# Feed-forward attention: the weighted values between the first two score tiles, the whole output product behind the fourth row's turns, the fourth score tile last

## What is computed

```
q = (h @ wq + bq).reshape(S, N_HEADS, HEAD_DIM)        # and kk, v; then the rotation
att = jnp.einsum('shd,thd->hst', q, kk) / np.sqrt(HEAD_DIM)
att = jnp.where(causal[None], att, jnp.finfo(att.dtype).min)
att = jax.nn.softmax(att, axis=-1)
attn_out = jnp.einsum('hst,thd->shd', att, v).reshape(S, N_HEADS * HEAD_DIM) @ wo
x1 = x + attn_out
h2 = _rms_norm(x1, ln2_w)
mlp = jax.nn.silu(h2 @ w_gate) * (h2 @ w_up) @ w_down
```

## Time and profile before

| | |
|---|---|
| median of 3 runs | 1528.08 us (1525.26 to 1529.14) |
| the profiled execution's own time | 1524.64 us |
| its span in the profile | 1522.9 us |
| TensorE busy | 1497.2 us, 98% |
| VectorE busy | 1182.6 us, 78% |
| ScalarE busy | 715.8 us, 47% |
| GpSimd busy | 688.5 us, 45% |
| attention of the second layer | scores from 1249 us on, the last output product until 1393 us |

### The profile page before, as it was taken

One profiled execution on the slowest core, in us unless ns is written; L12 is line 12 of the kernel. 1 busy time (PEld: TensorE's weight loads), 2 busy tenths in 40 slices (PEclk: granted clock), 3 DMA queues, 4 the chain that ended last, 5 costly groups with the idle time before them and its releaser, 6 DMA issues.

```text
span 1522.9 us, 41381 instructions
## 1 busy us (share of the span) xinstructions
PE 1497.2 (98%) x16220; PEld 1186.7 (78%) x16220; DVE 1182.6 (78%) x1884; ACT 715.8 (47%) x1458; POOL 688.5 (45%) x727
## 2 busy tenths in 40 slices
PE   8999999999999999999999999999999999999997
PEld 6777777777777777777777777777777787778997
DVE  6765788888888888888888888888887686554986
ACT  5874444444444444444444444444445124655431
POOL 3543344454444454444444444544445692114752
PEclk9999999999999999999999999999999999999999
DMA  8961121211111221112221112121125524010000
GB/s 262 346 207 60 39 63 52 77 56 50 56 54 59 67 66 50 56 50 62 62 70 50 56 50 62 58 75 50 56 87 154 196 111 167 28 56 29 1 1 25
DMA packets 70199, 121.04 MB, mean 79 GB/s; under 512 B 21840, under 2 KB 36528, under 8 KB 68608
## 3 DMA queue, kind: packets, MB, share of 16 engines
q1 hardware_dynamic: 69312, 117.54, 23.9%
q0 software_dynamic: 832, 2.75, 0.7%
HBM read 89.93 MB, written 30.34 MB: 79 GB/s over the span
## 4 chain that ended last, share of the span: by engine, by line
PE 89%; DVE 5%; ACT 3%; issue 1%; DMA 1%; POOL 1%; ACTq 0%; DVEq 0%; POOLq 0%
PE ps L1535 21%; PE ps L1536 19%; PE ps L1537 18%; PE ps L1691 10%; PE ps L1654 6%; PE ps L1625 3%; PE ps L1596 3%; PE ps L1660 2%; PE ps L1900 2%; PE ps L1917 2%; PE ps L1909 1%; PE ps L1664 1%; DMA q_dram<-q_turned 1%; DVE rec L1163 1%; PE ps L1636 0%
## 5 line engine op out<-in xcount | busy, mean ns | idle before, releaser
L547 POOL TENSOR_TENSOR ctx_lo<-ctx_raw,ctx_hi 128x472 fp32r<-128x472 f32 (+1 forms) x62 | 112.8, 1819 | 192.8 <-ACT ctx_hi L780 192.8
L1163 DVE RECIPROCAL rec<-ps 128x224 f32<-128x224 f32 x128 | 198.3, 1549 | 1.1 <-PE ps L1691 0.9
L581 POOL TENSOR_TENSOR prob_img<-prob 128x448 f32<-128x448 f32 x93 | 107.9, 1160 | 149.3 <-ACT prob L845 149.3
L1152 DVE TENSOR_REDUCE top<-ps 112x4 f32<-112x1028 f32 x128 | 156.2, 1220 | 0.0
L1151 DVE TENSOR_REDUCE top<-ps 112x4 f32<-112x472 f32 x128 | 83.1, 649 | 72.9 <-PE ps L1625 72.9
L1654 PE MATMUL ps<-q_all,k_all 32*128 32x112 f32 (+1 forms) x3072 | 125.2, 274 | 0.0
L1535 PE MATMUL ps<-w_v_img_hi,ctx_hi 128*128 128x512 f32 x256 | 107.4, 419 | 0.0
L1535 PE MATMUL ps<-w_k_img_hi,ctx_hi 128*128 128x512 f32 x256 | 107.1, 418 | 0.0
L843 ACT ACTIVATE prob<-ps 119x448 f32<-119x448 f32 x96 | 52.4, 546 | 114.8 <-PE ps L1654 114.8
L1654 PEld LDWEIGHTS ps<-q_all,k_all 32*128 32x128 f32 (+1 forms) x3072 | 105.4, 184 | 0.0
L1536 PE MATMUL ps<-w_k_img_lo,ctx_hi 128*128 128x512 f32 x256 | 101.1, 395 | 0.0
(11 more groups left out here) (358 smaller groups left out, 4410.7 us busy)
## 6 DMA issues: line engine op xcount, KB each, us to landing
ctx_raw<-in_ctx_dram SPq DMA_DIRECT2D x32, 748.0 KB, 4.2
xh_dram<-xh SPq DMA_DIRECT2D x32, 448.0 KB
xc<-in_xT_dram SPq DMA_DIRECT2D x28, 256.0 KB, 4.5
q_dram<-q_turned SPq DMA_DIRECT2D x28, 256.0 KB, 4.6
q_all<-q_dram SPq DMA_DIRECT2D x32, 224.0 KB, 3.1
out_dram<-out_sb SPq DMA_DIRECT2D x32, 224.0 KB, 2.3
xh<-in_x_dram SPq DMA_DIRECT2D x31, 224.0 KB, 2.9
proj<-in_x_dram SPq DMA_DIRECT2D x21, 256.0 KB, 5.1
```

The lines of the kernel that those rows point to most:

```text
L547: nc.gpsimd.tensor_tensor(ctx_lo[:, :, cols], ctx_raw[:, :, cols], ctx_hi[:, :, cols].bitcast(F32), ALU.subtract).then_inc(ctx_lo_done, 1)
L581: nc.gpsimd.tensor_tensor(prob_img[:, g % 2], image[:, 0, :], image[:, 1, :], ALU.add).then_inc(img_summed, 1)
L1152: nc.vector.tensor_reduce(rows[:, :, 2 * g + 1], ps[0:L, 2:6, TAIL:CTX], AX.X, ALU.max).then_inc(s_done, 1)
L1163: nc.vector.reciprocal(rec[:], bank[:, 2:4]).then_inc(norm_step, 1)
```

## The change

It writes the same instructions in another order, on three engines; none is added or removed.

TensorE, heads from 2 on: `weigh(h - 2)` goes from before the first score tile to between the first and the second. The turn of the second tile of the head before goes ahead of the first score tile, and the turn of the first tile ahead of the fourth score tile, which comes last. The output product stays one piece behind the turn of the fourth tile.

The diff:

```diff
--- before.py
+++ after.py
@@ -1046,32 +1046,53 @@
                     act.wait_ge(down_step, j - 2)
                 nc.scalar.activation(m_hi[:, j % 3, :], m_prod[:, j % 2, :], ACT.Copy).then_inc(m_hi_done, 1)
 
-            for k in range(FH * NC + LAG + 2):
-                if k % NC == 0 and k >= 2 * NC:
-                    attn_rounded(k // NC - 2)
-                if LAG <= k < FH * NC + LAG:
+            def prob_exp(k):
+                c = k % NC
+                n_keys = (c + 1) * L
+                act.wait_ge(top_ready, k + 1)
+                if k < AMONG:
+                    act.wait_ge(head_ready, NHEAD - 2 * AMONG + k + 1)
+                if k > LAG:
+                    act.wait_ge(pT_full, k - LAG)
+                nc.scalar.activation(prob2[:, k % (LAG + 1), 0:n_keys], ps[0:L, 4 + k % 2, 0:n_keys], ACT.Exp, bias=neg_top[:, c:c + 1],
+                                     accum_out=prob_sum[:, c:c + 1]).then_inc(prob_ready, 1)
+
+            for k in range(2 * NC):
+                if k >= LAG:
                     turn_evac(k - LAG)
-                if k < FH * NC:
-                    c = k % NC
-                    n_keys = (c + 1) * L
-                    act.wait_ge(top_ready, k + 1)
-                    if k < AMONG:
-                        act.wait_ge(head_ready, NHEAD - 2 * AMONG + k + 1)
-                    if k > LAG:
-                        act.wait_ge(pT_full, k - LAG)
-                    nc.scalar.activation(prob2[:, k % (LAG + 1), 0:n_keys], ps[0:L, 4 + k % 2, 0:n_keys], ACT.Exp, bias=neg_top[:, c:c + 1],
-                                         accum_out=prob_sum[:, c:c + 1]).then_inc(prob_ready, 1)
-                if k == 24:
+                prob_exp(k)
+                if k == NC + 2:
+                    wo_rounded(0)
+            attn_rounded(0)
+            prob_exp(2 * NC)
+            turn_evac(2 * NC - 3)
+            for h in range(2, FH):
+                k = NC * h
+                if h >= 3:
+                    turn_evac(k - 3)
+                    prob_exp(k)
+                    attn_rounded(h - 2)
+                if h == 6:
                     act.wait_ge(gate_step, NC)
                     nc.scalar.activation(gate_e[:], sel_score[:], ACT.Exp, scale=-1.0).then_inc(gate_exp, 1)
-                if k % NC == 2 and 1 <= k // NC <= FH:
-                    wo_rounded(k // NC - 1)
-                if k == FH * NC + LAG:
-                    act.wait_ge(att_full, FH * NC)
-                    act.wait_ge(ring_loaded[0], 48)
-                    act.wait_ge(ring_loaded[1], 32)
-                    gate_up_rounded(0)
-                    gate_up_rounded(1)
+                prob_exp(k + 1)
+                turn_evac(k - 2)
+                prob_exp(k + 2)
+                wo_rounded(h - 1)
+                turn_evac(k - 1)
+                turn_evac(k)
+                prob_exp(k + 3)
+            turn_evac(FH * NC - 3)
+            attn_rounded(FH - 2)
+            turn_evac(FH * NC - 2)
+            turn_evac(FH * NC - 1)
+            wo_rounded(FH - 1)
+            act.wait_ge(att_full, FH * NC)
+            act.wait_ge(ring_loaded[0], 48)
+            act.wait_ge(ring_loaded[1], 32)
+            gate_up_rounded(0)
+            gate_up_rounded(1)
+            attn_rounded(FH - 1)
 
             for kc in range(KC):
                 at = FH + FKV + KC + kc
@@ -1437,10 +1458,13 @@
 
             for k in range(FH * NC + LAG + 3):
                 c = k % NC
+                sooner = c in (0, 3) and k >= 2 * NC + 3
+                if sooner and k <= FH * NC:
+                    scale_probs(k - 1)
                 if k < FH * NC:
                     dve.wait_ge(att_full, k + 1)
                     nc.vector.tensor_reduce(neg_top[:, c:c + 1], ps[0:L, 4 + k % 2, 0:(c + 1) * L], AX.X, ALU.max, negate=True).then_inc(top_ready, 1)
-                if 1 <= k <= FH * NC:
+                if 1 <= k <= FH * NC and not sooner:
                     scale_probs(k - 1)
                 if k < 2:
                     rope(NHEAD - AMONG + k)
@@ -1936,23 +1960,33 @@
                     last.then_inc(o_step, 1)
 
             pe.wait_ge(consts2, 2)
-            for k in range(FH * NC):
-                if k % NC == 0 and k >= 2 * NC:
-                    weigh(k // NC - 2)
+            for c in range(AMONG):
+                att(c)
+                project_head(NHEAD - AMONG + c)
+            turn_probs(0)
+            for k in range(NC, 2 * NC):
                 att(k)
-                if k < AMONG:
-                    project_head(NHEAD - AMONG + k)
-                if k >= LAG:
-                    turn_probs(k - LAG)
-                if k % NC == 2 and 2 * NC <= k < FH * NC - NC:
-                    output_T(k // NC - 2)
-                elif k == FH * NC - 2:
-                    output_T(FH - 3, first)
+                turn_probs(k - LAG)
+            weigh(0)
+            att(2 * NC)
+            turn_probs(2 * NC - 3)
+            for h in range(2, FH):
+                k = NC * h
+                if h >= 3:
+                    turn_probs(k - 3)
+                    att(k)
+                    weigh(h - 2)
+                att(k + 1)
+                turn_probs(k - 2)
+                att(k + 2)
+                turn_probs(k - 1)
+                output_T(h - 2, range(KC) if h < FH - 1 else first)
+                turn_probs(k)
+                att(k + 3)
+            turn_probs(FH * NC - 3)
             weigh(FH - 2)
-            turn_probs(FH * NC - 3)
-            output_T(FH - 3, range(2, 3))
             turn_probs(FH * NC - 2)
-            output_T(FH - 3, range(3, KC))
+            output_T(FH - 3, second)
             turn_probs(FH * NC - 1)
             output_T(FH - 2, first)
             weigh(FH - 1)
```

## The result

| | before | changed |
|---|---|---|
| median | 1526.81 us (1525.26 to 1529.14, 4 runs) | 1546.26 us (1544.81 to 1548.0, 4 runs) |
| profiled execution | 1524.64 us | 1544.97 us |
| span | 1522.9 us | 1543.2 us |

What follows compares the result with a forecast made beforehand. TensorE, busy 1497.2 of 1522.9 us, was taken as the bound. Terms 16.1 + 1.0 - 0.4 gave +16.7 us: 1541.3 from the profiled 1524.64, 1544.8 from the median 1528.08; forecast 1544.5 us, range 1538 to 1550.

Steps and rivals of the forecast that it cites:

- The mechanism: In each head, ScalarE's three-block copy waits behind the second tile's exponential; the four-block turn waits 1.66 us instead of 0.15.
- 13 periods: From the first head's output product to the loop's last: 13 heads, each 1.24 us longer, together 16.1 us.
- The first output product: Ahead of the first output product the copy is held once, so it starts later: +1.0 us.
- Behind the loop: After the loop, the weighted values between two turns cover a head's two old waits: -0.4 us, an estimate.
- The clock: TensorE's granted clock in the attention stage was to stay 1.00, 2.4 GHz, adding nothing.
- Rival (c): TensorE's clock falls to 1.2 GHz for a tenth of 14 heads' matmul work: 1555 us, chance 0.05.
- Ahead of the stage: Before the feed-forward attention stage nothing was to move by more than 1 us.
- (a): In each head `attn_hi` starts 0.28 us sooner, wait 1.38: +0.96 a head, +13.1 in all, 1541 us; chance 0.11.
- (b): ScalarE's three-block copy isn't held, four-block wait stays 0.15: 3.9 us gained, 1524 us, or 1522 without that wait; chance 0.06.

Runs made afterwards that it cites:

- the first experiment: Changed kernel with ScalarE's copy of the three-block turn ahead of the second tile's exponential again, also before the loop: 1525.96 us, ratio 0.9993.
- the better order: Changed kernel with each ScalarE copy of a turn ahead of the next exponential and VectorE's order as before: 1522.75 us, ratio 0.9976.
- VectorE's edit undone: Changed kernel with the fourth tile's scaling behind the first tile's maximum again on VectorE: 1541.75 us, ratio 1.0096.
- the rest repaired: Changed kernel with ScalarE's copy ahead of the exponential everywhere except where the first output product waits for it: 1529.92 us, ratio 1.0024.
- ScalarE alone: Kernel before with only ScalarE's loop as changed, TensorE and VectorE as before: 1553.74 us, ratio 1.0196.
- the maximum ahead: Changed kernel with the second tile's maximum taken ahead of `attn_lo` on VectorE, ScalarE's order as changed: 1532.75 us, ratio 1.004.

## Why the prediction was right, and where it was off

*The mechanism held, step by step.* From the fourth tile's mask (1339.08) the prediction had the first tile's exponential at 2.55, `attn_hi` at 2.90, `attn_lo` at 3.48, the maximum at 4.01, the exponential at 4.43, the copy at 4.87, the four-block turn at 5.46. Measured: 2.53, 2.88, 3.44, 3.99, 4.40, 4.84, 5.42. TensorE was ready at 3.80, as worked out. The wait is 1.62 for 1.66, the head 9.14 for 9.17. The experiments show each link: with the copy moved the wait goes (0.18), with `attn_lo` moved it is 0.73, with the scaling moved 1.41.

*The terms of the sum*, for the two profiled executions, which differ by 20.3 us:

- 13 periods: 16.1 predicted, 13 x 1.21 = 15.7 measured.
- The first output product: +1.0 predicted; from the first score tile to its start 22.75 us before and 23.77 after, +1.0.
- Behind the loop: -0.4 predicted, about -0.6 measured (second product to the MLP's first matmul +13.9, less 12 periods, 14.5).
- **The clock: 0 predicted, +1.6 measured.** This is the step that failed. The prediction held that the clock "stays 1.00", since the first 10 us of the trace had TensorE 28% idle at full clock, which it took for "short idles of a larger share". That is a misreading. Of its 2.79 us of idle time 2.71 are one spell before TensorE's first matmul of the execution (the line below), so the row shows nothing of several waits close together. For the regular wait of each head that was right: 1.62 of 9.14 us, and the clock was 1.00. But around the first product three waits come close together, 2.67 us within 1270.9 to 1275.4, and the clock fell once. The prediction had costed the first head only by how late its product starts, and had not laid its waits beside each other. Rival (c) was there; what came was a sixth of its price. The Trainium skill, "TensorE: Matmul & The Clock Gate", section "A second HAM failure mode: psum-queue depth-cycling", tells of such falls from many short idles; the trace agrees at the first product, and disagrees in the heads that follow, where one wait of 1.62 us in each 9.14 us left the clock at 1.00.

```profile
2.71 3.67 PE L1698 MATMUL ps<-ident 128*128 128x128 f32 x16 [2.71 <-POOL rms_eps L609]
```

- Ahead of the stage: the prediction said that nothing moves by more than 1 us. The first score tile came at 1251.97 instead of 1249.31, +2.7. No code differs there. Laid beside the kernel before, matmul by matmul (both have 16220, in the same order up to the stage), the changed kernel is 1.0 us late at 150 us and 2.7 us late from 163 us on. The 1.7 between are the clock, which was at half around 160 us, in the layer before, and in the profile of the kernel before was not:

```profile
160.00:161.00 1.00, 1.00 (x32) 1.00 (x26) 0.52 (x1) 0.00 (x0) 0.00 (x0) 0.50 0.06 16
```

That fall is in six of the ten profiled executions of this case, always between 157 and 163 us, 1.7 us of clock each; it comes with the execution and not with the change. Nearly all of the 1.0 us comes in the first 110 us, where the ten profiled executions lie up to 1.7 us apart although none has other code there; what makes them differ stays open. Both blur whatever two medians of few runs say of 2 us: the stage's own distances in the trace are the finer measure.

The forecast of 1544.5 us lies 1.8 us under the median. Its 16.7 us are 15.7 + 1.0 - 0.6 = 16.1 in the trace, plus the 1.6 of the clock and the 2.7 ahead of the stage. A part of the closeness is luck: between the medians the change cost 19.5 us, 2.8 more than the sum, but the base that was added to it, 1527.8, lay 1.0 above the 1526.81 that the kernel before has over four runs.

*The rivals.* (a), the shorter chain, was what happens when VectorE's edit is taken out: 1.41 us of wait where 1.38 stood. Its 1541.75 us meet the 1541 of the rival in part by luck, being 14.9 over the kernel before and not 13.1, with one fall of the clock that the rival didn't have. (b), the copy that isn't held, is what the first experiment and the better order make: 0.9 and 4.0 us under the kernel before, where 3.9 stood, or 5.9 if the last 0.15 us of wait went too. It did not go (0.18 and 0.17), and the first experiment has the two waits at the one-block turn besides. In the changed kernel the order forbids (b).

## What to carry to other kernels

When a producer is moved later on one engine, follow its results through the other engines' lists, and look there for instructions that are ready but stand behind one that waits for the moved work. Here a copy of 0.44 us, ready for 1.5 us, held a whole output product. In a hand-written pipeline the copy that frees a shared bank goes ahead of an exponential that waits for another engine, and a new order on one engine is judged only with the orders of the others that fit it: alone TensorE's costs 7 us, ScalarE's 27, the two together 15, with VectorE's 19, and with a ScalarE order that fits it TensorE's gains 4.

## What the runs showed of the hardware

TensorE's clock can fall from waits of which none is above 1.2 us. It fell in every profiled kernel with the three waits of 0.8, 0.65 and 1.2 us before the first product (changed, VectorE's edit undone, the rest repaired, ScalarE alone), and in none of the six without them, one of which (the maximum ahead) had three of 0.8, 0.65 and 0.7 us. In that one's five timed runs the mean granted clock was 0.996 or 0.997, about as low as in the changed kernel's four (0.995 to 0.997), so the clock may have fallen in executions of which there is no trace. With 1.62 us of one wait in every 9.14 us it stayed at 1.00 in all heads; with 0.27 and 1.68 us in 9.46 (ScalarE alone) it fell in three heads of that run. A fall cost 1.6 us (the first product of the changed kernel, a head of 11.02 instead of 9.46 with ScalarE alone) to 2.7 us (the rest repaired: its 3.7 us less the 1.0 by which its product is late without it).

How an execution starts moves it by more than a small change does: in the first 110 us ten executions with the same matmuls lay up to 1.7 us apart.
